# Re-timing the row scatters of the last two batches, and pairing the others, in an attention and top-2 expert layer

## The reference

```
x = x + attention(layernorm(x))      # 16 heads of 8, causal softmax, projection Wo + bo
z = layernorm(x)                     # 4096 tokens of width 128
probs = softmax(z @ gate_w.T)        # 8 experts, the two largest per token are used
hidden = relu(z @ w1[e] + b1[e])     # 128 -> 512
y      = hidden @ w2[e] + b2[e]      # 512 -> 128
x = x + sum over the two experts of prob * y
```

## Time and profile before

| what | value |
|---|---|
| median of 3 runs | 552.78 us |
| the profiled execution, its own time | 552.5 us |
| its span, first to last instruction | 550.7 us |
| PE, DVE, ACT, POOL busy | 87%, 75%, 66%, 52% |
| attention, up to the last weighted sum | 0 to 362.0 us |
| slots 0 to 70 | 362.0 to 537.6 us |
| last stores, loads and sums | to 550.7 us |

### The profile page before, as it was taken

One profiled execution on the slowest core, in us unless ns is written; L12 is line 12 of the kernel. 1 busy time (PEld: TensorE's weight loads), 2 busy tenths in 40 slices (PEclk: granted clock), 3 DMA queues, 4 the chain that ended last, 5 costly groups with the idle time before them and its releaser, 6 DMA issues.

```text
span 550.7 us, 14537 instructions
## 1 busy us (share of the span) xinstructions
PE 480.7 (87%) x4337; PEld 342.9 (62%) x4337; DVE 413.0 (75%) x1282; ACT 362.7 (66%) x786; POOL 288.1 (52%) x583
## 2 busy tenths in 40 slices
PE   2789999999999999999998999867986889998980
PEld 1545656556556556556555556347876879998970
DVE  5888878988888888988979888724867435556884
ACT  8566776777777777776766667744664557776650
POOL 4603444535756656656655755674354644554441
PEclk9869999999999999999999999997998989999996
DMA  7334233132243243243233236521222222227453
GB/s 216 113 96 131 57 108 93 54 113 85 69 127 90 71 126 91 72 124 91 72 118 94 68 98 181 170 70 46 60 64 68 79 64 70 71 68 232 124 154 95
DMA packets 49741, 54.94 MB, mean 100 GB/s; under 512 B 6851, under 2 KB 41841, under 8 KB 49664
## 3 DMA queue, kind: packets, MB, share of 16 engines
q1 hardware_dynamic: 45312, 45.44, 28.6%
q0 software_dynamic: 4320, 8.47, 4.5%
q10 hardware_dynamic: 32, 0.10, 0.1%
HBM read 34.96 MB, written 17.90 MB: 96 GB/s over the span
## 4 chain that ended last, share of the span: by engine, by line
PE 65%; DVE 14%; ACT 7%; issue 6%; DMA 3%; another core or an unknown queue 2%; SPq 1%; DVEq 1%; POOL 0%; ACTq 0%; POOLq 0%
PE psO L986 13%; PE psS L958 9%; PE psT L1143 8%; PE psT L970 7%; DVE nmax L1295 7%; PE psO L1157 6%; PE psM L1157 5%; PE psS L960 3%; PE psS L1143 3%; PE psM L1006 2%; ACT PT L772 2%; PE psM L997 1%; PE psS L1133 1%; ACT shiftT L784 1%
## 5 line engine op out<-in xcount | busy, mean ns | idle before, releaser
L1295 DVE TENSOR_REDUCE nmax<-psS 128x1 f32<-128x512 f32 (+3 forms) x352 | 215.3, 633 | 43.5 <-PE psS L960 40.2
L772 ACT ACTIVATE PT<-psT 128x512 f32<-128x512 f32 x320 | 173.6, 598 | 78.5 <-PE psO L986 48.5
L958 PE MATMUL psS<-Ks,Qs 96*128 96x128 bf16 (+3 forms) x512 | 134.8, 308 | 7.9 <-DVE nmax L1295 3.8
L579 POOL TENSOR_SCALAR_AFFINE_SELECT PT<-PT 128x512 f32<-128x512 f32 x128 | 79.5, 636 | 109.7 <-ACT PT L772 108.5
L657 POOL DMA_INDIRECT token_y<-Qs,y_row x71 | 70.6, 995 | 84.6 <-DVE Qs L1631 49.7
L970 PE MATMUL psT<-Qs,Ks 108*128 108x384 bf16 (+3 forms) x512 | 108.4, 299 | 4.1 <-ACT PT L772 2.9
L960 PE MATMUL psS<-mask_qk,identb 128*128 128x128 bf16 x512 | 100.9, 223 | 0.0
L958 PEld LDWEIGHTS psS<-Ks,Qs 96*128 96x128 bf16 x512 | 50.3, 98 | 44.7 <-DVE nmax L1295 24.8
L986 PE MATMUL psO<-PT,Vs 128*32 128x512 f32 (+3 forms) x1024 | 76.0, 436 | 0.8 <-DVE x_all L1319 0.6
L606 POOL DMA_INDIRECT sorted_x<-xn,place x64 | 64.0, 1000 | 18.8 <-issue 16.4
L856 ACT ACTIVATE krest<-psT,turned 128x128 f32<-128x128 f32 x142 | 44.4, 363 | 30.5 <-PE psS L1143 10.7
(11 more groups left out here) (249 smaller groups left out, 679.3 us busy)
## 6 DMA issues: line engine op xcount, KB each, us to landing
Qs<-q_parts SPq DMA_DIRECT2D x96, 96.0 KB
Ks<-k_parts SPq DMA_DIRECT2D x95, 96.0 KB
xs_t<-sorted_x SPq DMA_DIRECT2D x71, 65.0 KB
w_sb<-in_L_ffn_w SPq DMA_DIRECT2D x16, 256.0 KB
q_parts<-qparts SPq DMA_DIRECT2D x32, 96.0 KB
k_parts<-kparts SPq DMA_DIRECT2D x8, 384.0 KB, 2.7
x_all<-in_L_attn_x SPq DMA_DIRECT2D x8, 256.0 KB, 4.7
v_all<-token_y SPq DMA_DIRECT2D x4, 512.0 KB
```

What stands on the lines that cost most here:

```text
L579: pool.affine_select(out=square, in_=square, compare_op=ALU.is_ge, fill=0.0, base=0, pattern=[[0, GH], [1, P]], channel_multiplier=-1).the ...
L772: act.activation(PT[:, n * T:(n + 1) * T], psT[:, bank, :], ACT.Exp).then_inc(prob_done[bank], 1)
L958: pe.matmul(psS[:, bank, c0:c0 + n], Qs[0:QK_ROWS, g, h, j * P:n], Ks[0:QK_ROWS, g, h, 0:n], start=True, stop=False)
L1295: dve.tensor_reduce(nmax[:, par, j, h:h + heads], src, AX_X, ALU.max, negate=True)\
```

## The change

It does four things. (1) In the attention steps the two scatters of a step, one at its end and one in the middle of the next, are issued as a pair at its end. (2) The eight scatters of batch 6 and the eight of batch 7 go to slots 3 to 18, one a slot after that slot's `store_y`; the one left over of batch 5 goes to the last attention step. (3) The four `normalise` of batch 6 go from before slot 0 to slots 2 and 3 on ACT. (4) DVE's last root step, offset and three `place_rows` instructions of batch 6 go from the end of the last attention step to slots 0 and 1.

```diff
-TAIL = dict(heads=0, norm=0, sorted6=1, attention=1, copy_attention=1, project=2, add=2,
+TAIL = dict(heads=0, norm=0, place6=0, finish6=1, sorted6=1, normalise6=2, attention=1, copy_attention=1, project=2, add=2,
...
-SCATTERS = {slot: number for number, slot in enumerate(range(10, 26, 2))}
+SCATTERS = {slot: number for number, slot in enumerate(range(3, 19))}
...
# GpSimd, in step(b, g)
-                if b >= 2 and g > 0:
-                    scatter(b - 2, 2 * g - 1)
-                if b >= 3 and g == 0:
-                    scatter(b - 3, CH * TOPK - 1)
...
                 if b >= 2:
                     scatter(b - 2, 2 * g)
+                    scatter(b - 2, 2 * g + 1)
...
# GpSimd, after the steps
-            scatter(BATCH - 3, CH * TOPK - 1)
-            for number in range(CH * TOPK):
-                scatter(BATCH - 2, number)
             for i in range(NSLOTS):
                 store_y(i)
                 if i in SCATTERS:
-                    scatter(BATCH - 1, SCATTERS[i])
+                    scatter(BATCH - 2 + SCATTERS[i] // (CH * TOPK), SCATTERS[i] % (CH * TOPK))
...
# ScalarE, before slot 0
-            for c in range(CH):
-                normalise(BATCH - 2, c)
...
# ScalarE, in slot i
-                if 0 <= i - TAIL["normalise"] < 2:
-                    for c in range(2):
-                        normalise(BATCH - 1, 2 * (i - TAIL["normalise"]) + c)
+                for b, slot in ((BATCH - 2, TAIL["normalise6"]), (BATCH - 1, TAIL["normalise"])):
+                    if 0 <= i - slot < 2:
+                        for c in range(2):
+                            normalise(b, 2 * (i - slot) + c)
...
# VectorE, in the last attention step
-                        if last and a == 10:
-                            for part in range(3):
-                                refine_roots(b - 1, 2, part)
-                            offset_roots(b - 1)
-                            for part in range(3):
-                                place_rows(b - 1, part)
...
# VectorE, tail(i)
+                if i == TAIL["place6"]:
+                    for part in range(3):
+                        place_rows(b - 1, part)
+                if i == TAIL["finish6"]:
+                    for part in range(3):
+                        refine_roots(b - 1, 2, part)
+                    offset_roots(b - 1)
```

## The result

The changed kernel took 565.98 us (median of 4 runs, 564.49 to 566.89) against 552.64 for the kernel before on the same chip: ratio 1.0247, interval 1.0208 to 1.0286, 2.5% slower. The prediction was 548, with 540 to 560 as its range. Its first rival, that the pairs hold PE's signals in the attention, had come true.

What follows compares the result with a forecast made beforehand. PE was taken as the bound (busy 87% of the span), its signals late while POOL issues indirect DMAs back to back. From 552.5 us: -8.4 - 7.6 + 7.6 + 4.0 + 0 = -4.4, so 548.1, said as 548; range 540 to 560.

Steps and rivals of the forecast that it cites:

- (e): Attention: 24 pairs of scatters over six batches were taken to cost 0, range -2.4 to +21.6 us.
- rival 1: Attention: the pairs hold PE's signals; 558.9 us at half its bound, 569.7 at the full bound; chance 0.19.
- (c): Slots 3 to 10: eight scatters added at +0.95 us each, +7.6 us; bounds +0.4 and +1.85 each.
- (a): Before slot 0 and to slot 3: ten scatters become two, -8.4 us; bounds -5 and -10.
- (d): Slots 11 to 18: eight scatters instead of four, +1.0 us for each more, +4.0 us; bounds +1.6 to +7.4.
- (b): Slots 19 to 29: four scatters go, 19.0 us instead of 26.60, -7.6 us; bounds -4.5 and -7.6.
- (f): Batch 5's leftover scatter, slot 33's wait for scatters, and DVE instructions taken from the last attention step: all hidden.
- Rival 2: Slots: a scatter in every slot acts like the burst, 1.85 us for each of 12, +22.2: 558.7 us; chance 0.15.
- Rival 3: Slots: most holds fall where nothing is due, 0.4 us for each of 12, +4.8: 541.3 us; chance 0.13.
- Rival 4: First slots: late signals belong to first use of expert code or weights, not POOL; about 552 us; chance 0.07.

Runs made afterwards that it cites:

- e10: The kernel before with only the attention's scatters put in pairs, against the kernel before: 567.53 us against 553.92, ratio 1.0256.
- e11: The changed kernel with the attention scatters single again, against the kernel before: 551.54 us against 553.92, ratio 0.9973.

## Why the prediction was wrong

**Step (e), the pairs, failed.** I took 0 with bounds of -2.4 and +21.6, and the attention lost 16.6 us in the first profile and 12.5 with pairs only: 0.7 and 0.5 us for each of 24 pairs, against my 0.9 at the full bound. The wait that I had put at nothing is that of ACT and DVE for PE's signals behind a pair. The mechanism was in the text as rival 1, with its place (0.9 to 2.8 us after the first issue; the trace has 3.0) and its point of decision (0.2 us a pair). What misled me was the row that I called nearest: expand(0), ended at 364.90 in the burst and answered at once. The same burst held the next signal for 5.6 us, so one answered signal showed only that not every one is held. Rows 8, a store behind a scatter with PE's signal 2.2 us late, were the like case, two issues and not ten. Rows 9, which price single scatters at 0.06 us, said nothing of two. And my cycle in (c), with signals held until 0.8 to 1 us behind the last issue, fits a pair but not the burst it was set beside: there the first held signal was let go at 371.54, with issues still to come until 373.84.

**Step (a), the burst, was right:** copy_y of slot 0 came 4.66 us after the last copy, and 8.4 us were saved to there, 9.2 to slot 3 where I had 8.4, since slots 0 to 3 took 7.0 us and not 8.3. That the burst caused the wait is shown by the set of e10 and e11: 12.95 us with it and 4.69 without, on one chip in one hour (the second also has ACT's four normalise moved, which I had put at 0.4). In the other condition the burst costs nothing (4.63 with it and 4.66 without).

**Steps (c) and (d), scatters in slots 3 to 18,** +7.6 and +4.0: measured +9.1 and +2.5 in the changed kernel, +8.5 and +3.0 without pairs. The sum of 11.6 is the sum measured (11.6 and 11.5), but that is partly luck: the first term was 1.5 too small and the second 1.5 too large.

**Step (b), slots 19 to 29,** -7.6: measured -4.9 and -5.0. I priced ten slots at PE's pace. Even in the other condition they take 19.8 to 19.9 us and not 19.0; and in both held profiles slots with a store alone still take up to 4.4 and 3.7 us behind the last scatter, which stands in slot 18. The measured size lies near the bound of -4.5. From slot 29 on I had forecast no change: so it was without pairs (37.91), but not in the profiled execution of the changed kernel (+2.6), which was its longest.

**Step (f)** held: without pairs slots 29 to 49, slot 33 among them, took 37.91 us as before.

**Rivals 2 to 4.** Rival 2 (a scatter in each slot acts like a burst, 1.85 each) is refuted by 27.31 and 26.74 us. Rival 3 (0.4 each) too, in the held condition; in the other it is nearly right: slots 3 to 11 take 18.34 us in the changed kernel against 18.22, slots 11 to 19 take 22.96 against 22.07. Rival 4 was the most instructive. By the rule of the Trainium skill that the prediction cites ("SBUF — State Buffer", "Who interferes with whom"), PE waits on no DMA, and I took from it that a burst could not delay PE's signals. In five of six sets the traces agree with that. In the first measurement and in the set of e10 and e11 they don't, by 8.4 us at one place. The rule itself speaks of the ports of SBUF and not of signals, so whether it or only my use of it fails is not shown. I gave it 0.07 as a cause elsewhere; what I had not thought of is that both are true at different times.

My sum with the pairs as measured is 548.1 + 12.5 to 16.6 = 561 to 565; the chip gave 566.

**A better version.** The change without pairs is better than the changed kernel, and level with before: with held signals the ratio is 0.9973 (0.9915 to 1.0032), without 0.9994 to 1.0018. No version measured here beats the kernel before.

**Open.** What makes PE's signals late in one hour and not in another on the same chip (the granted clock of the attention is 0.99 to 1.00 in both, and DMA moves the same 54.94 MB); whether it is the issue on GpSimd or the transfer of the rows that goes with the late signals, which no run separates; and whether spacing the pair, or another place for it, would help there. The held condition was met twice only, in the first measurement and in the set of e10 and e11.

## What to carry to other kernels

When a profile shows signals that arrive long after the instruction that sent them, the price read from it belongs to that condition: have the kernel before measured at another time before tuning against it, for here a gain of 8.4 us and a loss of 16.6 existed only in one of two. To price an arrangement that the trace does not show, take the row in which the same signals are due at the same moment, not the row that looks alike. And keep indirect DMAs on GpSimd from standing back to back where the path waits for PE's signals: in the held condition single scatters cost some 0.1 us each in the attention (5.3 / 48, of which 3.4 us in batches 5 and 6), a pair 0.5 to 0.7 more than the two scatters apart, and ten in a row 8.4.

## What the hardware showed that I had not expected

- The same program took 529 us and 554 us on the same chip 19 minutes apart, with DVE's, ACT's and POOL's work within 2.3 us in the profiles of either condition; the difference lies where indirect DMAs are issued, with PE's signals up to 5.6 us late.
- Behind a pair the held signals are let go together, about 0.8 us after its last issue ended (178.48 to 179.25; 176.68 to 177.44). Behind ten in a row it is otherwise: a first release comes 10.03 us after the first issue, with issues still to come (361.51 to 371.54; 374.05 to 384.08 with pairs only), and the next one 2.0 us after the last issue ended (DVE at 375.80 and 388.39). What sets these times is open.
- With held signals stores can fall into pairs though each slot has one. In the profile of the changed kernel, from slot 21 to slot 48, two stores are issued back to back and every second slot takes about 3 us, the others about 1 (POOL in order of time):

```profile
485.68 0.98 POOL L652 DMA_INDIRECT token_y<-Qs,y_row  x1 [1.82 <-DVE Qs L1616]
486.97 0.98 POOL L652 DMA_INDIRECT token_y<-Qs,y_row  x1 [0.30 <-issue]
489.68 0.98 POOL L652 DMA_INDIRECT token_y<-Qs,y_row  x1 [1.73 <-DVE Qs L1616]
```

Slots 29 to 49 took 2.6 us longer there than before. In the kernels without pairs and with pairs only, under the same condition, the pattern had ended by slot 29 (37.91 and 37.92 us). No run took it apart.
